# A convolution and window-attention kernel: another order of one turn of the attention, and the masked copies of pooled v on GpSimd

## What is computed

```python
# layer 0: group norm, then a 3x3 convolution
x = x + conv3x3(gn(x), L0_conv_weight)                # 256 -> 256 channels
# layer 1: group norm, then linear attention in windows of 4x4 tokens, projection, batch norm
xw  = windows(gn(x))                                  # 8 images x 196 windows of 16 tokens
qkv = einsum('nchw,oc->nohw', xw, qkv_w)              # 32 heads of q, k and v, 8 wide
msq = concat([qkv, avg_pool5(qkv)])                   # 32 plain heads and 32 pooled ones
kv  = relu(k).T @ [v, 1]                              # 8 x 9 for each head and window
out = relu(q) @ kv;  out = out[:, :8] / (out[:, 8] + 1e-15)
x = x + batch_norm(proj_w @ out)
```

## Time and profile before

| what | value |
|---|---|
| median of 3 runs | 2531.64 us (2530.62 to 2537.7) |
| the profiled execution | 2529.08 us, its span 2527.1 us |
| granted TensorE clock | 0.999 of full speed |
| PE busy | 2464.9 us (98%) |
| ACT busy | 1497.3 us (59%) |
| DVE busy | 1726.4 us (68%) |
| POOL busy | 787.7 us (31%) |
| DMA | 57.74 MB, 23 GB/s on average |

### The profile page before, as it was taken

One profiled execution on the slowest core, in us unless ns is written; L12 is line 12 of the kernel. 1 busy time (PEld: TensorE's weight loads), 2 busy tenths in 40 slices (PEclk: granted clock), 3 DMA queues, 4 the chain that ended last, 5 costly groups with the idle time before them and its releaser, 6 DMA issues.

```text
span 2527.1 us, 113160 instructions
## 1 busy us (share of the span) xinstructions
PE 2464.9 (98%) x49568; PEld 2156.1 (85%) x49568; DVE 1726.4 (68%) x3609; ACT 1497.3 (59%) x3952; POOL 787.7 (31%) x2164
## 2 busy tenths in 40 slices
PE   4999999999999999999999999999999999999999
PEld 4998889888898888988889888998889978898887
DVE  8876658766587666866668666686666866665665
ACT  2148871488615885168851688427883278823887
POOL 0014430244302443034420444204441044401444
PEclk9999999999999999999999999999999999999999
DMA  4000010000100001000010000100001000000000
GB/s 163 1 2 15 19 59 12 2 18 15 65 6 5 15 18 67 1 5 19 15 67 1 9 15 17 65 1 9 19 15 63 1 13 19 15 9 2 15 19 19
DMA packets 38933, 57.74 MB, mean 23 GB/s; under 512 B 4688, under 2 KB 36304, under 8 KB 36560
## 3 DMA queue, kind: packets, MB, share of 16 engines
q1 hardware_dynamic: 38736, 55.27, 6.2%
HBM read 29.57 MB, written 25.69 MB: 22 GB/s over the span
## 4 chain that ended last, share of the span: by engine, by line
PE 96%; ACT 1%; DVE 1%; issue 1%; DMA 0%; POOL 0%; SPq 0%; POOLq 0%; DVEq 0%
PE ps L319 33%; PE ps L390 16%; PE ps L338 11%; PE ps L365 10%; PE ps L379 9%; PE ps L345 8%; PE ps L354 5%; PE ps L399 3%; ACT ve L568 1%; ACT ve L558 0%; PE ps L304 0%; DMA xs<-w_conv 0%; PE ps L507 0%; DVE st L717 0%; DVE kv_part L867 0%
## 5 line engine op out<-in xcount | busy, mean ns | idle before, releaser
L319 PE MATMUL ps<-dp,wc 128*128 128x392 f32 x4608 | 834.0, 341 | 2.0 <-issue 2.0
L319 PEld LDWEIGHTS ps<-dp,wc 128*128 128x128 f32 x4608 | 816.4, 188 | 3.2 <-issue 2.3
L894 DVE TENSOR_TENSOR kvm<-ps,hm 128x576 f32<-128x576 f32 (+1 forms) x400 | 296.3, 741 | 387.0 <-PE ps L365 386.8
L540 ACT CAST dp<-dt 128x896 fp32r<-128x896 f32 x128 | 120.9, 945 | 558.4 <-PE ps L319 468.0
L1044 POOL TENSOR_TENSOR qm<-qraw 128x64 f32<-128x64 f32 x200 | 61.6, 308 | 1242.8 <-ACT qraw L579 1242.8
L390 PEld LDWEIGHTS ps<-at,wp 128*128 128x128 f32 x3200 | 372.7, 191 | 43.8 <-issue 41.4
L390 PE MATMUL ps<-at,wp 128*128 128x128 f32 (+1 forms) x3200 | 409.2, 281 | 0.4 <-ACT at L603 0.4
L1073 POOL TENSOR_TENSOR xs<-yb,xs 128x128 f32<-128x128 f32 (+3 forms) x560 | 207.3, 397 | 415.4 <-ACT yb L595 415.4
L338 PE MATMUL ps<-wkv,xt 128*128 128x512 f32 x1200 | 331.7, 411 | 0.4 <-ACT ve L568 0.4
L558 ACT ACTIVATE ve<-ps,vmask 128x256 f32<-128x256 f32 x800 | 314.8, 492 | 0.0
L568 ACT ACTIVATE ve<-ps,vmaskp 128x256 f32<-128x256 f32 x800 | 313.4, 484 | 0.0
(11 more groups left out here) (87 smaller groups left out, 2882.7 us busy)
## 6 DMA issues: line engine op xcount, KB each, us to landing
out<-xs SPq DMA_DIRECT2D x224, 112.0 KB, 1.8
xs<-x SPq DMA_DIRECT2D x16, 1344.0 KB, 8.7
xs<-x SPq DMA_DIRECT2D x16, 224.0 KB, 2.7
xs<-w_conv SPq DMA_DIRECT2D x1, 2304.0 KB, 8.5
kvm<-w_kv SPq DMA_DIRECT2D x1, 512.0 KB, 14.4
wp<-w_proj SPq DMA_DIRECT2D x4, 128.0 KB, 8.0
wq<-w_q SPq DMA_DIRECT2D x1, 256.0 KB, 13.9
gav<-gavg SPq DMA_DIRECT2D x1, 64.0 KB, 8.2
```

The lines of the kernel that those rows point to most:

```text
L319: last = nc.tensor.matmul(ps[:, BANK_C[kk % 2][mt], 0:CONV_N], wc[:, part_w, k, kt * TAPS + dy, mt * P:(mt + 1) * P], dp[:, kk % 2, part_d ...
L894: nc.vector.tensor_tensor(kvm[:, h, 0:n].rearrange("p r (g c) -> p r g c", g=2), ps[:, BANK_A + 2 * h:BANK_A + 2 * h + n, 0:2 * PLACES * Q ...
```

## The change

Turn s of TensorE becomes: attend of tile s; both keys-times-values of tile s+1; q of tile s+2; transposes of tile s; pooling of tile s+2; projection of tile s-1; k and v of tile s+3. The other engines' orders follow, and tiles are prepared further ahead (tile s+4 is normalized in turn s). The projection gets free columns of the banks of keys-times-values, and `yb` a second buffer. The hardware loop has 20 turns in place of 22. The first chunk of the next image's convolution now takes in more of the first tiles, and the two halves of one convolution product are put into the last two turns of an image. Pooled v leaves PSUM in one ScalarE copy (`vpraw`); GpSimd multiplies it by the masks into `ve` for all four places in one instruction (`spread_pooled`).

```diff
 # TensorE
-            def tile(T, e, s=None):     # old body, the order above
+            def tile(T, e, s=None, v=None):
...
+                pe.wait_ge(masked, masks)
+                pe.wait_ge(q_ready, n1)
+                pe.wait_ge(qp_ready, n1)
+                if is_tile(-1):
+                    pe.wait_ge(at_ready, n0)
+                attend(e, units(0))
+
+                if is_tile(1):
+                    pe.wait_ge(v_ready, n2)
+                    if is_tile(-2):
+                        pe.wait_ge(y_ready, n0)
+                    keys_times_values(0, 1 - e, units(1))
+                    pe.wait_ge(vp_ready, n2)
+                    keys_times_values(1, 1 - e, units(1))
+
+                if is_tile(2):
+                    pe.wait_ge(q_ready, n2)
+                    q_of_tile(e)
+                if v is not None and not is_tile(2):
+                    if is_tile(1):
+                        pe.wait_ge(q_ready, n2)
+                        product(v, 0)
+                    else:
+                        pe.wait_ge(vp_raw, n1)
+                        product(v, 1)
+                pe.wait_ge(ao_ready, n1)
+                turn(units(0))
+                if is_tile(2):
+                    pooled(n3)
+                if is_tile(-1):
+                    if is_tile(1):
+                        pe.wait_ge(masked, own_mask)
+                    else:
+                        pe.wait_ge(y_ready, n0)
+                    project(1 - e, 2)
+                if is_tile(3):
+                    pe.wait_ge(xh_low, n4)
+                    pe.wait_ge(vp_raw, n3)
+                    keys_values(n4, 1 - e)
 # ScalarE
             def pooled_keys_values(b, t):
                 act.wait_ge(pool_done, b * TILES + t + 1)
                 nc.scalar.activation(kr[:, t % 2, C:2 * C], ps[0:TT, BANK_KV, 0:C], ACT.Relu, scale=POOL_SCALE)
-                for e in range(PLACES):
-                    last = nc.scalar.activation(
-                        ve[:, t % 2, e, 1].rearrange("p (n m) -> p n m", m=DIM + 1)[:, :, 0:DIM],
-                        ps[0:TT, BANK_KV, C:2 * C].rearrange("p (n m) -> p n m", m=DIM),
-                        ACT.Copy, scale=vmaskp[:, e:e + 1])
-                last.then_inc(vp_ready, 1)
+                if b or t:
+                    act.wait_ge(vp_ready, b * TILES + t)
+                nc.scalar.activation(vpraw[:], ps[0:TT, BANK_KV, C:2 * C], ACT.Copy, scale=POOL_SCALE).then_inc(vp_raw, 1)
...
             def attention(b):
-                for s in range(TILES): ...
+                for s in range(-1, TILES):
+                    if s >= 0:
+                        turned(b, s)
+                    if 0 <= s < TILES - 2:
+                        pooled_keys_values(b, s + 2)
+                    if s + 2 < TILES:
+                        q_of_tile(b, s + 2)
+                    if s >= 1:
+                        batch_norm(b, s - 1)
+                    if s + 4 < TILES:
+                        split_tile(b, s + 4)
+                    if s + 3 < TILES:
+                        keys_values(b, s + 3)
 # VectorE
             def attention(b):
+                normalize_tile(b, 3)
+                tile_low(b, 3)
                 for s in range(TILES):
-                    mask(b, s, 0) ... outputs(b, s)    # old order: see the kernel
+                    weights(b, s)
+                    outputs(b, s)
+                    if s + 2 < TILES:
+                        kv_low_part(b, s + 2)
+                    if s + 1 < TILES:
+                        mask(b, s + 1, 0)
+                        mask(b, s + 1, 1)
+                        pooled_q(b, s + 1)
+                    if s + 4 < TILES:
+                        normalize_tile(b, s + 4)
+                        tile_low(b, s + 4)
 # GpSimd
+            def spread_pooled(b, t):
+                pool.wait_ge(vp_raw, b * TILES + t + 1)
...
+                nc.gpsimd.tensor_tensor(
+                    ve[:, t % 2, :, 1].rearrange("p e (n m) -> p e n m", m=DIM + 1)[:, :, :, 0:DIM],
+                    vpraw[:].rearrange("p (n m) -> p n m", m=DIM).unsqueeze(1).to_broadcast([TT, PLACES, C // DIM, DIM]),
+                    vmask[:].unsqueeze(2).unsqueeze(3).to_broadcast([TT, PLACES, C // DIM, DIM]),
+                    ALU.mult).then_inc(vp_ready, 1)
...
+                for s in range(-1, TILES):
+                    if 0 <= s < TILES - 2:
+                        spread_pooled(b, s + 2)
+                    if s + 2 < TILES:
+                        pool_q(b, s + 2)
                     if 1 <= s:
                         add_tile(b, s - 1)
```

More of the change, by code:

```diff
@@ L401, in turn, with is_tile, units @@
                     last.then_inc(tr_done, 1)
-            def tile(T, e, s=None):
[L405 to L434, removed]
+            def tile(T, e, s=None, v=None):
+                def is_tile(d):
+                    return s is None or 0 <= s + d < TILES
+                def units(d):
+                    return 2 if s is None else tile_units(s + d)
+                n0, n1, n2, n3, n4 = [held(pe, T + d) for d in range(5)]
+                masks, own_mask = held(pe, T * 2 + 2), held(pe, T * 2 + 3)
                 pe.wait_ge(w_loaded, DMA)
@@ L453, in attention @@
+                pe.wait_ge(vp_raw, t0 + 2)
+                keys_values(t0 + 3, 0)
+                if b + 1 < B:
+                    pe.wait_ge(conv_added, 2 * v + 4)
+                for s in range(FIRST_LOOPED):
+                    tile(t0 + s, s % 2, s)
                 with pe.Fori(0, LOOPED // 2) as i:
[L454 to L457, removed]
+                    for e in range(2):
+                        tile(t0 + i * 2 + (FIRST_LOOPED + e), (FIRST_LOOPED + e) % 2)
@@ L459, in last_tile @@
+                for s in range(FIRST_LOOPED + LOOPED, TILES):
+                    tile(t0 + s, s % 2, s, v)
             def last_tile(b):
@@ L522, in _ @@
                     first_tile(b)
[L523 removed]
+                    keep_warm(WARM_TILE)
                     pooled(b * TILES + 1)
+                    second_tile(b)
+                    keep_warm(WARM_TILE)
+                    pooled(b * TILES + 2)
                 attention(b)
[L526 to L527 removed]
             last_tile(B - 1)
@@ L1032, in _ @@
                     kv_low_part(b, 0)
+                    normalize_tile(b, 2)
+                    tile_low(b, 2)
+                    kv_low_part(b, 1)
+                    mask(b, 0, 0)
+                    mask(b, 0, 1)
                     pooled_q(b, 0)
@@ L1079, in _ @@
                 pool_q(b, 0)
-                for s in range(TILES):
-                    if s + 1 < TILES:
-                        pool_q(b, s + 1)
+                spread_pooled(b, 0)
+                spread_pooled(b, 1)
+                for s in range(-1, TILES):
[3 more added lines that the diff above has]
+                        pool_q(b, s + 2)
                     if 1 <= s:
```

118 lines of the change are left out of this document (65 added, 53 removed).

## The result

The changed kernel takes 2489.93 us (median of 4 runs, 2486.85 to 2494.62) against 2531.13 us of the kernel before on the same chip: a ratio of 0.9833 (95% interval 0.9809 to 0.9857), 41 us faster. The forecast was 2515, with a range of 2410 to 2565. The direction was as forecast, and so was the place where GpSimd holds VectorE up; the gain is more than twice the 16 us of the sum, so terms of the sum are wrong and have to be found.

The account below looks back on a forecast made before the run. TensorE bounded the kernel at 8.12 us a turn. Per image, -16.6 (trips) - 1.5 (idle) + 2 (waits) + 21 x (8.10 - 7.43) = -2.0 us, over eight images -16: 2513 profiled, 2515 median; range 2410 to 2565.

Parts of the forecast that it names:

- the 16 us of the sum: Whole run: -2.0 us per image from trips, idle, new waits and lengthened turns; 16 us less over eight images.
- The turn without new waits: TensorE's steady turn with one stretch of small matmuls: 7.43 us of blocks, 0.69 less than before, 7.5 with the mask wait.
- Both trips: TensorE's two saved round trips between small and wide matmuls per turn: 0.345 us each, 0.69 together.
- The block of VectorE for a whole long instruction: GpSimd's new multiplication in spread_pooled holds the shared port, delaying VectorE's normalizing of tile s+4; chance that this paces a faster kernel 0.48.
- Rival A: GpSimd's long multiplication doesn't block VectorE: turn 7.5 us, time 2415 us; chance 0.20.
- B: Rival: slower, as spread_pooled's multiplication costs more per element; 2.4 ns per element gives 2574 us; chance 0.18.
- 1024 x 2.1 ns = 2.1 us held: GpSimd's new multiplication holds the port 2.1 us, at a price read from 128 and 96 elements; row some 2.3 us long.
- the loop of 8.10: From pooling to pooling through blocked normalizing, rounding, k and v copies and low part: 8.10 us, in 21 of 25 turns.
- Idle gone ahead of attend: 11.6/8 = 1.5 us per image: At an image's ends, TensorE's idle time ahead of attend vanishes: 1.5 us less per image.
- new waits I take as 2 us: Per image, new waits in turn 22 and the fuller first chunk: 2 us, bounds 0 and 4.
- The convolution halves cover the dividing chain: In an image's last two turns, the halves of a convolution product hide the dividing chain; no size given.
- theory F: From the experiments, not the forecast: part of the gain is lost to instruction fetches outside running loops and the lowered clock.

Follow-up runs that it names:

- experiment 7: Changed kernel with q put between attend and keys-times-values in all turns, so two stretches of small matmuls per turn; 2488.61 us, 0.984 of the kernel before.
- experiment 1: Changed kernel, but GpSimd's long multiplication waits until VectorE has normalized tile t+2; 2483.22 us, 0.9806 of the kernel before.
- 9: Changed kernel with GpSimd's multiplication waiting for normalizing, and q between attend and keys-times-values in the five written-out turns alone; 2462.58 us, 0.974 of the kernel before.
- experiment 5: Changed kernel with turns 1 and 2 written out too, leaving 18 turns in the loop in place of 20; 2504.83 us, 0.9913 of the kernel before.
- experiment 8: Changed kernel with both convolution halves behind an image's last turn instead of inside the last two; 2510.32 us, 0.9924 of the kernel before.
- 4: Changed kernel with one more GpSimd multiplication of 512 elements, into a spare buffer, ahead of each spreading; 2569.94 us, 1.0164 of the kernel before.

## Why the prediction was right in direction and wrong in size

**Right.** The turn without new waits: forecast 7.43 of blocks and 0.06 of waiting for the mask, measured 7.54. Attend is 1.14 (forecast 1.08), keys-times-values 1.16 (1.15), q with transposes 1.35 (1.36), pooling 0.55 (0.56), projection 1.80 (1.70 and 0.06), k and v 1.54 (1.58). Attend and keys-times-values do join. Both trips together are 8.12 - (7.54 - 0.09) = 0.67, forecast 0.69; experiment 7 prices the one with q alone at 0.24. The block of VectorE for a whole long instruction was there, at the place that was named: GpSimd started 1.50 behind pooling (forecast 1.53). Rival A, no block, is thereby wrong (experiment 1), and so is B: the price per element is lower and not higher than taken. The Trainium skill ("SBUF — State Buffer", "SBUF: two separate sides") has the lock exclusive for whole instructions, and these runs agree with it at 1024 elements. The Trainium skill's page "GPSIMD Engine Reference" (3.1, Elementwise) gives 4497 ns for an addition of 2048 elements, as an estimate 2.2 ns each; this multiplication took 1961/1024 = 1.9 ns.

**Wrong, first: the hold, and how it enters the turn.** "1024 x 2.1 ns = 2.1 us held" was an extension of two sizes of at most 128 elements. Measured: 1.79 us, 1.75 ns per element, in a row of 1.96 us in place of 2.3. The release came at 3.29 behind pooling in place of 3.73, and the additions between, for which I took 0.1, cost nothing. Normalizing was done at 4.0 on average (3.85 with two pieces, 4.22 with four) in place of 4.60. The 0.6 less makes the loop of 8.10 one of about 7.35 in short turns and 7.7 in long ones. And the mean was the wrong thing to work with. A turn takes the longer of TensorE's blocks and the loop, for each kind of tile: in four of seven TensorE's 7.54 decides and the block costs nothing, in three the loop decides, 7.7, and pooling, once it has had to wait, takes 0.11 more to the projection's start, 7.80. Why it does is open; in the turn of before, behind attend, it took the same 0.66. That gives 7.65 in place of 8.10, and 21 x 0.45 x 8 = 76 us less than the forecast: 2439 us. The rows of before already had both kinds of tiles apart, as the forecast itself said.

**Wrong, second: stops for instructions, a term that the sum put at nothing.** "Idle gone ahead of attend: 11.6/8 = 1.5 us per image" and "new waits I take as 2 us" come to 4 us more idle time in the whole run. TensorE's idle time grew by 34 us, from 62.2 to 96.2. The waits are not what was missed: 7.7 of the 11.6 us were waits for the mask in turn 0 and are gone, as forecast, and the new ones (nine of 0.79 us) come to less than the 16 us taken, so that all idle time that is no stop fell by 5 us. But the other 3.8 us of that row were stops, as in the timeline of before, which cuts attend after 124 of its 128 matmuls:

```profile
802.20 1.26 PE L379 MATMUL ps<-kvm,qs 64*32 64x36 f32 x124
804.53 0.26 PE L379 MATMUL ps<-kvm,qs 64*32 64x36 f32 x4 [1.06 <-issue]
```

I had read "issue" as one kind of wait, which would go with its neighbour. The change raised the stops from 6.3 to 45.2 us, 39 more, as it puts up to 192 small matmuls with as many weight loads behind each other and writes out more turns; the first of these two reasons is borne out by experiments 7 and 9, the second shown by experiment 5. The 30 us of idle time over the forecast, and 24 us more at half the clock, worth about 12, are 42 of the 51 us between 2437 (the corrected sum for the profiled execution) and 2488; the other 9 I can't place.

**Too small: the halves.** "The convolution halves cover the dividing chain" was right in its place, but I gave the cover no price; without it the change would gain 20 us and not 41 (experiment 8).

The two errors have opposite signs, -76 and +51. Each is larger than the gain that was forecast. That the time came within 25 us of 2515 is thus in part luck.

**What is shown, and what is argued.** The block is shown by taking it away (1) and by making it longer (4). That the stops come where text is new is shown by 5; that they wait for fetches rests on their ends, which keep one distance from a packet of q8 whatever their length, on the packets that grow with TensorE's text, and on their absence once the loop is in its second pass. No run takes the fetches away. Why q between relieves them is argued from theory F; that it does is measured (7 and 9). How much the clock takes is worked out from its time at half level, with no kernel that holds the clock alone.

## What to carry to other kernels

When a change lengthens one path and shortens another, work out each kind of turn by itself and take the longer path there; a mean over kinds puts a cost on turns in which it is hidden. Read every "issue" row of the chain by its place in the timeline: if it stands where the program waits, look for another engine's row that ends just ahead of its end, for it is then a plain wait; if it cuts a block in two and lies in written-out text or in a loop's first pass, it grows with the length of that text and with the number of small instructions behind each other, and a rearrangement that saves TensorE's time can pay it back there. Order a dense stretch one way inside a hardware loop and another way in the written-out turns if need be: here that was worth 18 us over the same kernel without it.

## What the runs showed of the hardware

- TensorE stopped for 0.4 to 2.1 us, and for 3.4 and 4.4 us while x was being loaded (at 283 GB/s around the longer one), mostly in stretches of small matmuls, in written-out turns and in the first pass of the loop: 29 stops of 45.2 us. No later pass had one. Each ended 1.25 to 1.55 us behind the end of a 16 KB packet of q8, of which one came for about 128 matmuls of written-out text.
- A row that the profile calls "issue" can be a wait for data: nine of 0.79 us ended 0.10 us behind ScalarE's copy, eight of 0.97 us in the kernel before 0.10 us behind VectorE's mask.
- Behind the longest stop TensorE ran at its lower level: 18 convolution matmuls took 5.1 us in place of 3.3.
- A GpSimd multiplication of 1024 elements per partition took 1.96 us and shut out VectorE's SBUF-to-SBUF work for 1.79 of them; with 512 elements ahead of it, normalizing ended 0.74 us later.
- Going from small to wide matmuls and back costs 0.24 to 0.34 us of TensorE's time, and no idle row shows it.
